# Attention steps written out straight, and value products that read v_all directly

## What is computed

```python
x = x + xattn(layernorm(x), ctx, ctx, mask)   # 16 heads of 8; scores / scale, masked, softmax, times values, Wo
x = x + ffn(layernorm(x))                     # router picks 2 of 16 experts (hidden 64), plus a shared expert
```

## Time and profile before

| | |
|---|---|
| Time, median of 3 runs | 195.28 us (194.29 to 195.44) |
| The profiled execution's own time | 196.06 us |
| Its span | 194.2 us |
| Mean granted clock of TensorE | 0.984 of full |
| Attention steps (first scores of step 0 to router of step 15) | 33.87 to 106.84 us |

### The profile page before, as it was taken

How to read it: one execution, slowest core, us unless ns; L and a number is a source line. 1 busy time by engine, 2 the same in 40 slices (tenths; PEclk the granted TensorE clock), 3 DMA queues, 4 the chain that set the end, 5 groups by cost and what they waited for, 6 DMA issues and landing times.

```text
span 194.2 us, 4355 instructions
## 1 busy us (share of the span) xinstructions
PE 178.0 (92%) x1351; PEld 129.6 (67%) x1351; DVE 169.3 (87%) x515; ACT 129.7 (67%) x296; POOL 93.0 (48%) x150
## 2 busy tenths in 40 slices
PE   7498599999999999999998789999999999999962
PEld 7465447566666666667666466778888878888841
DVE  6899999589999999999995699998899889988981
ACT  2196465888999889999895855566556655566641
POOL 6755992758888888889886781300000000000000
PEclk9999969999999999999999999999999999999997
DMA  5897800000000000000000153342363236333301
GB/s 125 273 263 154 326 6 0 2 3 0 5 0 5 0 0 0 0 0 3 2 3 2 40 207 131 98 134 72 117 190 127 71 114 178 123 76 126 124 0 54
DMA packets 13201, 15.31 MB, mean 79 GB/s; under 512 B 1665, under 2 KB 8193, under 8 KB 13057
## 3 DMA queue, kind: packets, MB, share of 16 engines
q1 hardware_dynamic: 12608, 14.57, 24.2%
q10 hardware_dynamic: 576, 0.55, 1.3%
HBM read 13.93 MB, written 1.18 MB: 78 GB/s over the span
## 4 chain that ended last, share of the span: by engine, by line
PE 61%; DVE 17%; issue 5%; ACT 3%; DMA 3%; DVEq 0%; POOL 0%; SPq 0%; POOLq 0%
PE bank L1035 26%; PE bank L989 13%; PE bank L971 5%; PE bank L980 5%; PE bank L929 3%; DVE hid L849 3%; ACT hid_hi L624 2%; DVE prob L785 2%; DVE smax L764 2%; PE bank L950 2%; DVE xn L675 2%; PE bank L960 2%; DVE cmix_sb L849 2%; DMA mix_all<-w_rows 2%; DVE hid_lo L841 1%
## 5 line engine op out<-in xcount | busy, mean ns | idle before, releaser
L615 ACT ACTIVATE sig<-bank 128x512 f32<-128x512 f32 x36 | 21.5, 600 | 20.9 <-PE bank L1035 20.3
L989 PE MATMUL bank<-k_blk,q_blk 128*128 128x512 f32 x64 | 34.0, 615 | 0.2 <-issue 0.2
L441 POOL TENSOR_TENSOR k_blk<-k_all,consts_sb 128x512 f32<-128x512 f32 x32 | 32.7, 1046 | 0.0
L1035 PE MATMUL bank<-xt_hi,w_hi 128*128 (+1 forms) x72 | 29.2, 405 | 0.0
L1035 PE MATMUL bank<-xt_lo,w_hi 128*128 (+1 forms) x72 | 28.4, 394 | 0.0
L1035 PE MATMUL bank<-xt_hi,w_lo 128*128 (+1 forms) x72 | 28.2, 392 | 0.0
L832 DVE TENSOR_TENSOR hid_u<-sig,bank 128x512 f32<-128x512 f32 x32 | 21.9, 684 | 4.1 <-PE bank L1035 2.5
L764 DVE TENSOR_REDUCE smax<-bank 128x8 f32<-128x512 f32 x32 | 21.9, 685 | 2.9 <-PE bank L989 2.9
L568 ACT COPY prob_t<-bank 128x512 f32<-128x512 f32 x32 | 18.8, 587 | 6.9 <-PE bank L971 6.9
L785 DVE TENSOR_TENSOR prob<-bank,smax 128x512 f32<-128x512 f32 x32 | 22.0, 686 | 0.6
L573 ACT ACTIVATE prob<-prob 128x512 f32<-128x512 f32 x32 | 20.8, 653 | 0.0
(11 more groups left out here) (118 smaller groups left out, 382.5 us busy)
## 6 DMA issues: line engine op xcount, KB each, us to landing
mix_all<-w_rows SPq DMA_DIRECT2D x64, 128.0 KB, 2.9
w_moe_sb<-w_moe SPq DMA_DIRECT2D x1, 1728.0 KB, 9.7
x_sb<-x SPq DMA_DIRECT2D x4, 256.0 KB, 7.8
ctxt_sb<-ctx_t SPq DMA_DIRECT2D x4, 256.0 KB, 6.1
ctx_sb<-ctx_nat SPq DMA_DIRECT2D x4, 256.0 KB, 5.3
out<-x_sb SPq DMA_DIRECT2D x3, 256.0 KB, 2.3
w_att_sb<-w_att ACTq DMA_DIRECT2D x1, 264.0 KB, 5.3
mrow<-mask_row ACTq DMA_DIRECT2D x1, 256.0 KB, 4.4
```

The source lines that it names most:

```text
L441: last = nc.gpsimd.tensor_tensor(k_blk[p][:, g, :, :], k_all[:, bass.ds(t, 1), g, :].broadcast_to([P, HG, S]), hmask_sb.rearrange("p (h o) ...
L615: nc.scalar.activation(sig[r][:, :], gate_ps[r][:, :], ACT.Silu).then_inc(s_sig, 1)
L989: nc.tensor.matmul(score_ps[g][:, :], q_blk[q][:, g, :, :].rearrange("p b s -> p (b s)"), k_blk[q][:, g, :, :].rearrange("p h s -> p (h s) ...
L1035: last = nc.tensor.matmul(out, w, moving, start=start and k == 0, stop=stop and k == 2)
```

## The change

The loop of `pipeline` is replaced by a plain Python loop: steps 0 to 15 are all written out, and every tile number is a constant. `v_blk`, its memsets, ScalarE's copy and the semaphores `s_vblk` and `s_vwide` go. The value products take the 18 columns of a pair in `v_all` as weights and write 18 rows of each group of 32 in `pvt_ps`; the other 14 rows keep what was there, and nothing reads their transposes. TensorE waits for `v_all` itself.

```diff
         def pipeline(eng, step):
-            start = TRAIL + 1
-            bodies = (TILES - 2 - start) // STEPS
-            end = start + bodies * STEPS
-            for t in range(LEAD + 1, start):
-                peel(step, t)
-            with eng.Fori(0, bodies) as i:
-                for k in range(STEPS):
-                    step(i * STEPS + (start + k), (start + k) % 2, lambda lag: True)
-            for t in range(end, TILES):
-                peel(step, t)
+            for t in range(LEAD + 1, TILES):
+                step(t, t % 2, lambda lag: 0 <= t - lag < TILES)
...
-            for p in range(2):
-                nc.gpsimd.memset(v_blk[p][:, :, :, :].rearrange("p b j w -> p (b j w)"), 0.0).then_inc(s_vwide, 1)
...
-                if on(-1):
-                    if isinstance(t, int) and t < 0:
-                        act.wait_ge(s_vwide, 2)
-                        act.wait_ge(s_vden, 2)
-                        act.wait_ge(s_v_sb, 1)
-                    elif isinstance(t, int) and t == 0:
-                        act.wait_ge(s_v_sb, GROUPS)
-
-                    nc.scalar.copy(v_blk[q][:, :, :, 0:2 * DV].rearrange("p b j w -> p (b j) w"),
-                                   v_all[:, bass.ds(t + 1, 1), :, :, :, :].rearrange("p o b j e d -> p (o b j) (e d)"))\
-                        .then_inc(s_vblk, 1)
...
                             last = nc.tensor.matmul(
-                                pvt_ps[c * PW:(c + 1) * PW, h * P + b * S:h * P + (b + 1) * S], v_blk[p][:, b, j, :],
+                                pvt_ps[c * PW:c * PW + 2 * DV, h * P + b * S:h * P + (b + 1) * S],
+                                v_all[:, t, b, j, :, :].rearrange("p e d -> p (e d)"),
                                 prob_t[p][:, j, b * S:(b + 1) * S], start=True, stop=True, tile_position=(0, c * PW))
...
                 if on(0):
-                    pe.wait_ge(s_vblk, t + 1)
+                    if t == 0:
+                        pe.wait_ge(s_vden, 2)
+                    if t % GT == 0:
+                        pe.wait_ge(s_v_sb, t // GT + 1)
                     values(0)
                     values(1).then_inc(s_pvt, 1)
```

More of the change, by code:

```diff
@@ L101, in build_program @@
         k_blk = [sb(f"k_blk{p}", [P, 2, HG, S]) for p in range(2)]
-        v_blk = [sb(f"v_blk{p}", [P, BPT, PAIRS, PW]) for p in range(2)]
         pvt_sb = sb("pvt_sb", [P, 2 * P])
@@ L180, in build_program @@
         s_blk = sem("s_blk")
-        s_vblk = sem("s_vblk")
         s_score = [sem(f"s_score{g}") for g in range(2)]
@@ L190, in build_program @@
         s_pv = sem("s_pv")
-        s_vwide = sem("s_vwide")
         s_iden = sem("s_iden")
```

## The result

The changed kernel takes 194.06 us (median of 22 runs, 193.52 to 195.14) against 195.28 (22 runs, 194.29 to 196.09): a ratio of 0.9945, 95% interval 0.9929 to 0.996. By the ratio that is 1.1 us less, between 0.8 and 1.4; the medians lie 1.22 us apart. The forecast was 194.5 us, 0.75 less. The runs of the changed kernel fall into two groups, 12 up to 194.13 us and 10 from 194.53 us on, so that a median moves with the number of runs in each.

What follows compares the result with a forecast made beforehand. The prediction took each step to be bound by a circle through VectorE, TensorE and one ScalarE copy. Gains of 0.71 (loop) and 0.04 us (copies) made 0.75, taking the median from 195.28 to 194.5 us, range 193.3 to 195.6.

Steps and rivals of the forecast that it cites:

- The loop: Steps 4 to 11: main term, with constants instead of registers 36.47 us fall to 35.76, a gain of 0.71 us.
- step 3: Step already written out before the loop, 4.47 us against 4.51 inside it; taken as the model for the looped steps.
- L945 starts 0.08 us after the attention: TensorE's transpose of the divided attention, inside a loop step: its start 0.08 us later was read as waiting for VectorE.
- the turn: Where the loop begins its next pass: scores start after 0.15 us in which TensorE waited for no engine; inside the 0.71.
- The rival that only the turn counts: Loop: registers do not lengthen steps, all eight take 4.51 us; 0.39 us gained, 194.9 us; chance 0.11.
- the rival of the fetch: Written-out steps: a fetch stall of 0.15 us in each of eight would cost 1.2 us, giving 195.7 us; chance 0.05.
- the rival of slower reads: Value products: reading `v_all` in pieces of 18 columns is slower, 6.1 us over 16 steps, 200.6 us; chance 0.06.
- The copies: ScalarE's 16 copies into `v_blk`: dropping them gains nothing inside the steps, covered by its wait; 0.04 us once at the start.
- Narrow weights: Value products with weights of 18 columns: gain between nothing and 0.7 us, taken as zero.
- 1.5 ns a column: TensorE's weight loads: 156 ns for 64 columns, 109 for 32, so 18 columns would be some 20 ns shorter.
- The prediction's limit, `xt2_hi` on ScalarE: Router start: it also needs `xt2_hi`, so faster products gain at most 0.05 us a step in steps 2 to 11.
- rival that narrow weights pay: Value products: their second half shrinks, 0.5 to 0.7 us more gain, 194.0 us or a little below; chance 0.23.

Runs made afterwards that it cites:

- experiment 1: The kernel before with only its loop written out, ScalarE's copies into `v_blk` and the 32 columns kept; 194.38 us, ratio 0.9944.
- experiment 9: The changed kernel with VectorE's steps 4 to 11 alone put back into the loop of two passes; 194.43 us, ratio 0.9964.
- experiment 10: The kernel of experiment 1 with TensorE's steps 4 to 11 alone put back into the loop of two passes; 195.38 us, ratio 1.0001.
- experiment 2: The kernel before, loop and copies kept, with value products taking only 18 of the 32 columns of `v_blk`; 194.84 us, ratio 0.9986.
- experiment 3: The changed kernel, but with the 18 columns taken from `v_blk`, so that ScalarE's copies and the memsets stay; 194.40 us, ratio 0.9954.
- experiment 11: The changed kernel with steps 4 to 11 of ScalarE and GpSimd put back into the loop of two passes; 194.74 us, ratio 0.997.
- experiment 4: The changed kernel with three ScalarE copies a step of 288 columns into a tile that nothing reads; 195.66 us, ratio 1.0015.
- experiment 5: The changed kernel with the value products reordered, the four column groups in turn, then the second batch; 194.08 us, ratio 0.9938.
- experiment 8: The kernel before with eight steps in the loop's body and one pass, copies and 32 columns kept; 194.89 us, ratio 0.998.

## Why the prediction was right

**The loop, 0.71 forecast, 0.76 measured.** The eight steps of the loop lost 0.69 us (36.47 against 35.78 in experiment 1), where 0.71 was forecast. The rest lies behind the loop, where the prediction had nothing: 0.04 in step 12, which is written out in both kernels, and 0.03 in steps 13 to 15. Experiments 9 and 10 share the term out: VectorE's loop 0.40 and TensorE's loop 0.39, together 0.79. The mechanism was the one read from step 3: VectorE's chain of small operations is longer in the loop, the attention comes later, and its transpose waits. One reading on the way was wrong: that L945 starts 0.08 us after the attention is no sign of a wait, since it starts right behind TensorE's own scores in both kernels; the sign is that it lasts 0.31 us and not 0.27. The chain is longer by one operation alone, the cast. The prediction had the turn inside the 0.71 and saw 0.15 us of it in TensorE's idle time; alone it is 0.32 us (4.79 against 4.47, experiment 10), and it is TensorE's. The rival that only the turn counts fell with experiment 9, the rival of the fetch with experiment 1, where straight code runs at 4.47 us a step throughout, and the rival of slower reads with experiments 2 and 3. The Trainium skill (Runtime: NRT & Kernel Launch, Instruction fetch mechanics) says that a taken branch whose target is not in the code already fetched has to wait for a fetch. The turn of 0.3 us would fit that, but no run shows a fetch, and the turns of the other three engines made no step longer (experiments 9 and 11); what the turn consists of stays open.

**The copies, 0.04 forecast, 0.04 measured**, by experiment 3 against the changed kernel. That the cover has an end is shown by experiment 4, and its size was wrong in my expectation there: it is ScalarE's idle time in both halves of the step, not in one, and the wait in the middle of the value products.

**Narrow weights, zero forecast between zero and 0.7; 0.16 measured.** This is the term that was mis-sized. It is 0.17 in the loop (experiment 2) and 0.16 written out (3 against 1), 0.01 us in nearly every step and 0.02 to 0.03 in step 15. The prediction took zero because the instructions are much closer together than a load is long; they got a little closer still. The load went from 109 to 97 ns, 12 for 14 columns. The Trainium skill (TensorE: Matmul & The Clock Gate, LDWEIGHTS) says that a load takes its number of columns divided by 1.2, in ns. The trace agrees with the slope of that between 32 and 18 columns, by an estimate 11.7 ns for 14, and not with the whole load: 97 ns is far more than 15. So the prediction's remark that no proportion shows was right, while its own 1.5 ns a column, read from another product's loads, was too steep. Thirty-two loads that are 12 ns shorter would make 0.38 us a step if they added up; the step got 0.01 us shorter. The prediction's limit, `xt2_hi` on ScalarE, is all but reached in experiment 5.

**The rest.** 0.76 + 0.16 + 0.04 = 0.96 us: the three kernels form a chain from the one before to the changed one, so their differences make up the stage's. The ratio of the runs says 0.8 to 1.4. The measured 194.06 us is the time that the prediction gave to its rival that narrow weights pay; that is chance, since these brought 0.16 us and not 0.5 to 0.7. In the two profiled executions the time after the last router is 0.24 us shorter too (194.2 - 106.45 against 192.9 - 105.39); experiment 11, whose steps end as those of the changed kernel, has 192.1 - 104.32 = 87.78, as long as before, so that I count this as difference between runs. The prediction had no term for the fall of the clock: it gave half a microsecond for the difference between runs and no cause.

## What to carry to other kernels

Follow the circle of one step through all engines before costing an edit: 5 us less work on ScalarE brought 0.04 us, and a small VectorE operation that came 0.1 us later in each of eight steps cost 0.4. Compare a loop's steps with the same steps written out next to it; the difference, and the turn, can be read before anything is changed. Where the runs differ by more than the edit, compare a stretch of the trace that the disturbance does not reach.

## What the hardware showed that I had not expected

- In looped steps one small VectorE operation, the cast, started 0.17 us behind the one ahead instead of 0.06 (experiments 9, 10), while `gap`, addressed by the same register, kept its 0.08. The loops of ScalarE and GpSimd cost the step nothing (experiment 11).
- A loop of a single pass left the trace of straight code, with 4.47 us a step, and of the loop only 0.06 us in the first step behind it (experiment 8).
- TensorE's clock fell to half in the projections in the profile of both kernels: once before, from 24 to 28 us, and twice in the changed kernel, from 9 to 13 and from 23 to 27 us. The four runs of the changed kernel whose granted clock was 1.0 took 193.52 to 193.63 us, the four at 0.976 to 0.978 took 194.68 to 194.83. That is as much as the whole change. In between, the mean clock does not order the runs (193.80 to 195.14 at 0.986). With 25 fill products of a constant six runs lay within 0.56 us.
